# Pair products of layer 0 for three tiles at once, spread over four steps; norms of layers 1 and 2 two steps later

## What is computed

```python
z = jnp.einsum('bmd,bhd->bdmh', x, prev).reshape(b, D, m * h)
t = jnp.einsum('bdc,co->bdo', z, ws[k]) + bs[k]
t = jnp.transpose(t, (0, 2, 1))
norm = jnp.sqrt(jnp.sum(t * t, axis=(-2, -1), keepdims=True))
t = t / norm
logit.append(t)
prev = t
```

## Time and profile before

| | us |
|---|---|
| median of 3 runs | 1061.17 (1060.83 to 1064.76) |
| the profiled execution: its own time | 1062.48 |
| the profiled execution: span | 1060.8 |
| PE busy / PEld busy | 1028.2 / 782.4 |
| DVE busy | 983.6 |
| POOL busy | 865.9 |
| ACT busy | 791.3 |

### The profile page before, as it was taken

How to read it: one execution, slowest core, us unless ns; L and a number is a source line. 1 busy time by engine, 2 the same in 40 slices (tenths; PEclk the granted TensorE clock), 3 DMA queues, 4 the chain that set the end, 5 groups by cost and what they waited for, 6 DMA issues and landing times.

```text
span 1060.8 us, 17970 instructions
## 1 busy us (share of the span) xinstructions
PE 1028.2 (97%) x4320; PEld 782.4 (74%) x4320; DVE 983.6 (93%) x3344; ACT 791.3 (75%) x2655; POOL 865.9 (82%) x729
## 2 busy tenths in 40 slices
PE   2999999999999999999999999999999999999998
PEld 0477777878777787877778787777878777788884
DVE  2589999999999999999999999999999999999993
ACT  3476877868788786868778687777868778788872
POOL 6777988889898888988888898888889888577770
PEclk9999999999999999999999999999999999999999
DMA  5650030302303030120303012030301203000000
GB/s 188 129 143 12 3 88 3 89 2 52 96 4 88 3 87 4 21 71 2 89 3 87 5 28 64 3 89 2 85 7 17 74 3 89 1 1 1 2 1 1
DMA packets 75892, 46.10 MB, mean 43 GB/s; under 512 B 55689, under 2 KB 58633, under 8 KB 75658
## 3 DMA queue, kind: packets, MB, share of 16 engines
q1 hardware_dynamic: 68487, 38.59, 15.2%
q10 hardware_dynamic: 2179, 5.07, 1.4%
q0 software_dynamic: 5120, 1.29, 1.4%
HBM read 42.99 MB, written 1.94 MB: 42 GB/s over the span
## 4 chain that ended last, share of the span: by engine, by line
PE 48%; POOL 19%; DVE 18%; issue 9%; ACT 5%; DMA 1%; POOLq 0%; DVEq 0%; SPq 0%; ACTq 0%
POOL sums L432 14%; DVE sums L946 12%; PE acc L778 8%; PE bank_d L722 7%; PE bank_d L723 6%; PE bank_d L724 6%; PE bank_a L724 6%; PE bank_a L722 6%; PE bank_a L723 6%; POOL gathered L415 5%; ACT scaled L560 4%; DVE bank_d L946 2%; DVE sums L965 1%; ACT sums L560 1%; PE turned L799 1%
## 5 line engine op out<-in xcount | busy, mean ns | idle before, releaser
L432 POOL TENSOR_TENSOR sums<-sums,scaled 128x512 f32<-128x512 f32 (+1 forms) x512 | 645.1, 1262 | 133.4 <-ACT scaled L560 97.4
L946 DVE SCALAR_TENSOR_TENSOR sums<-bank_d,x_col,sums 128x128 f32<-128x128 f32 x2304 | 654.2, 339 | 29.3 <-PE bank_d L724 20.2
L560 ACT ACTIVATE scaled<-bank_a,x_col 128x128 f32<-128x128 f32 x1920 | 551.5, 385 | 139.8 <-PE bank_a L724 132.7
L722 PE MATMUL bank_d<-w_hi,prev_lo 128*128 128x512 f32 x640 | 288.0, 450 | 6.2 <-DVE sums L965 4.7
L722 PE MATMUL bank_a<-w_hi,prev_lo 128*128 128x512 f32 (+1 forms) x640 | 263.9, 412 | 2.6 <-issue 1.3
L724 PE MATMUL bank_d<-w_hi,prev_hi 128*128 128x512 f32 x640 | 252.5, 394 | 0.0
L723 PE MATMUL bank_d<-w_lo,prev_hi 128*128 128x512 f32 x640 | 252.1, 394 | 0.0
L724 PE MATMUL bank_a<-w_hi,prev_hi 128*128 128x512 f32 (+1 forms) x640 | 245.3, 383 | 0.0
L723 PE MATMUL bank_a<-w_lo,prev_hi 128*128 128x512 f32 (+1 forms) x640 | 245.1, 383 | 0.0
L560 ACT ACTIVATE sums<-bank_a,x_col 128x128 f32<-128x128 f32 x512 | 146.1, 369 | 76.8 <-PE bank_a L724 75.9
L415 POOL DMA_INDIRECT gathered<-in_table,idx x160 | 177.2, 1108 | 28.5 <-issue 18.3
(11 more groups left out here) (84 smaller groups left out, 528.2 us busy)
## 6 DMA issues: line engine op xcount, KB each, us to landing
x_pairs<-x_scratch SPq DMA_DIRECT2D x135, 156.0 KB
x_pairs<-x_scratch SPq DMA_DIRECT2D x96, 78.0 KB
gathered<-in_table,idx POOLq DMA_INDIRECT x160
x_sq<-x_scratch SPq DMA_DIRECT2D x32, 64.0 KB
x_pairs<-x_scratch SPq DMA_DIRECT2D x92, 22.0 KB
x_scratch<-gathered SPq DMA_DIRECT2D x16, 72.0 KB
w_raw<-in_w ACTq DMA_DIRECT2D x1, 1024.0 KB, 5.1
w_raw<-in_w ACTq DMA_DIRECT2D x1, 896.0 KB
```

What stands on the lines that cost most here:

```text
L432: nc.gpsimd.tensor_tensor(out=sums[:, n % SUMS, 0:w, :], in0=sums[:, n % SUMS, 0:w, :], in1=scaled[:, a - 1, 0:w, :], op=ALU.add).then_inc ...
L560: op = nc.scalar.activation(to[:, i, :], bank_a[at % A_RING][:, i * UNITS:(i + 1) * UNITS], ACT.Copy, scale=x_of(c, q, a * PER_BANK + i))
L722: nc.tensor.matmul(to, lo, w_h, start=True, stop=False)
L946: nc.vector.scalar_tensor_tensor(out=taken(n, u) if u in LEFT else total, in0=taken(n, u), scalar=x_of(c, q, A_FIELDS + u), in1=total, op0 ...
```

## The change

Layer 0's products are made in two groups of three tiles instead of three groups of two. The first extra row set is loaded a third time to fill the last rows of the third tile, so that each DVE instruction takes all 128 rows. The PE tiles move to other places, the norm of layers 1 and 2 moves from s5/s6 to s7/s0 of the next iteration, and with it `high` and `low` of layer 2's input to (s1, 0); `turn_x` moves to (s2, 9), the reductions of layer 2 on DVE to (s1, 12) and (s1, 15). In chunk 0 all products are made tile by tile, and PE waits for each.

```diff
-EXTRA_PAIRS = [(0, 0, 1, FIELDS - 1), (2, 2 * EXTRA, 2 * EXTRA + 1, 2 * EXTRA - 1)]
+EXTRA_PAIRS = [(0, 0, 1, FIELDS - 1), (3, 2 * EXTRA, 2 * EXTRA + 1, 2 * EXTRA - 1)]
-PAIR_GROUPS = [[0, 1], [2, 3], [4, 5], [6]]
+PAIR_GROUPS = [[0, 1, 2], [3, 4, 5], [6]]
...
-        FINISHES.append((2, _it - 2, (step_at(_it, _q), 3), (step_at(_it, _q + 1), 3)))
+        FINISHES.append((2, _it - 2, (step_at(_it, _q), 3), (step_at(_it, _q + 1), 12 if _it < CHUNKS - 1 else 3)))
...
+    elif _it < CHUNKS:
+
+        NORMS.append((_items, (step_at(_it, 7), 7), (step_at(_it, 7), 3), (step_at(_it + 1, 0), 2)))
     else:
         NORMS.append((_items, (step_at(_it, 5), 7), (step_at(_it, 5), 3), (step_at(_it, 6), 2)))
...
-                    (step_at(_c, 7), 0) if _c < CHUNKS - 1 else (step_at(_c, 5), 3)
+                    (step_at(_c + 1, 1), 0) if _c < CHUNKS - 1 else (step_at(_c, 5), 3)
...
-        _first = (step_at(_it, 0), 2) if _it == 1 else (step_at(_it - 1, 7), 12)
-        _made = [_first, (step_at(_it, 0), 12), (step_at(_it, 1), 12 if _it > 1 else 17), (step_at(_it, 2), 5)]
-        _summed = {(step_at(_it, 0), 5): [0], (step_at(_it, 0), 8): [1], (step_at(_it, 1), 1): [2],
-                   (step_at(_it, 1), 4): [3], (step_at(_it, 2), 1): [4], (step_at(_it, 2), 4): [5],
-                   (step_at(_it, 2), 8): [6]}
+        _i = [step_at(_it, q) for q in range(3)]
+        if _it == 1:
+            _made = [(_i[0], 2), (_i[1], 4), (_i[2], 2)]
+            _summed = {(_i[0], 5): [0], (_i[0], 7): [1], (_i[0], 9): [2]}
+        else:
+            _last = step_at(_it - 1, 7)
+            _made = [(_last, 4), (_i[1], 4), (_i[2], 2)]
+            _summed = {(_last, 7): [0], (_last, 9): [1], (_i[0], 1): [2]}
+        _summed.update({(_i[1], 7): [3], (_i[1], 9): [4], (_i[2], 1): [5], (_i[2], 8): [6]})
...
-TURNS_AT = {((0, 12) if _c == 1 else (step_at(_c - 1, 1), 8)): _c for _c in range(1, CHUNKS)}
+TURNS_AT = {((0, 12) if _c == 1 else (step_at(_c - 1, 2), 9)): _c for _c in range(1, CHUNKS)}
...
-        PAIR_LOADS = [2 * PER_TILE + 3, 2 * PER_TILE + 3, PER_TILE, 0]
+        PAIR_LOADS = [2 * PER_TILE + 4, 2 * PER_TILE + 4, 0]
...
-            if p < 2:
-                tile, _, *partners = EXTRA_PAIRS[p]
-                for i, partner in enumerate(partners):
-                    if tile + i in tiles:
-                        load_rows(queue, c, p, x_rot[PAIR_ROWS:128, tile + i, :], partner, [[2 * ROWS, EXTRA]])
+            tile, _, *partners = EXTRA_PAIRS[p]
+
+            for i, partner in enumerate(partners + partners[:1]):
+                if tile + i in tiles:
+                    load_rows(queue, c, p, x_rot[PAIR_ROWS:128, tile + i, :], partner, [[2 * ROWS, EXTRA]])
...
-                if tile == PAIR_GROUPS[group][0]:
+                if c == 0 and tile in FIRST_SINGLY:
+                    pe.wait_ge(first_pairs_made, FIRST_SINGLY.index(tile) + 1)
+                elif c == 0 or tile == PAIR_GROUPS[group][0]:
                     pe.wait_ge(pairs_made, c * NP + group + 1)
...
-                if c == 0 and p < 2:
+                if c == 0:
+
                     for i in tiles:
                         if i < PICKED:
                             dve.wait_ge(picked, i + 1)
-                        mult = nc.vector.tensor_tensor(out=z0[:, i, :], in0=bank_d[i][:, :] if i < PICKED else x_rot[:, i, :],
-                                                       in1=x_reps[p][:, :], op=ALU.mult)
-                    mult.then_inc(pairs_made, 1)
+                        rows = 128 if i in WITH_EXTRA else PAIR_ROWS
+                        mult = nc.vector.tensor_tensor(out=z0[0:rows, i, :],
+                                                       in0=bank_d[i][0:rows, :] if i < PICKED else x_rot[0:rows, i, :],
+                                                       in1=x_reps[p][0:rows, :], op=ALU.mult)
+                        mult.then_inc(first_pairs_made if i in FIRST_SINGLY else pairs_made, 1)
                     return
-                nc.vector.tensor_tensor(out=z0[0:rows, tiles[0]:tiles[0] + count, :],
-                                        in0=x_reps[min(p, 1)][0:rows, :].unsqueeze(1).to_broadcast([rows, count, ROWS]),
-                                        in1=x_rot[0:rows, tiles[0]:tiles[0] + count, :],
+                nc.vector.tensor_tensor(out=z0[:, tiles[0]:tiles[0] + count, :],
+                                        in0=x_reps[p].unsqueeze(1).to_broadcast([128, count, ROWS]),
+                                        in1=x_rot[:, tiles[0]:tiles[0] + count, :],
                                         op=ALU.mult).then_inc(pairs_made, 1)
```

More of the change, by code:

```diff
@@ L29 @@
 EXTRA = 128 - PAIR_ROWS
-EXTRA_PAIRS = [(0, 0, 1, FIELDS - 1), (2, 2 * EXTRA, 2 * EXTRA + 1, 2 * EXTRA - 1)]
+EXTRA_PAIRS = [(0, 0, 1, FIELDS - 1), (3, 2 * EXTRA, 2 * EXTRA + 1, 2 * EXTRA - 1)]
 SQUARES = PAIR_TILES
-PAIR_GROUPS = [[0, 1], [2, 3], [4, 5], [6]]
+PAIR_GROUPS = [[0, 1, 2], [3, 4, 5], [6]]
 NP = len(PAIR_GROUPS)
+WITH_EXTRA = [first + n for first, _, *partners in EXTRA_PAIRS for n in range(len(partners))]
 PICKED = 3
@@ L279, in cin_kernel @@
         pairs_made = sem("pairs_made")
+        first_pairs_made = sem("first_pairs_made")
         pairs_summed = sem("pairs_summed")
@@ L317, in cin_kernel @@
         y_stored = sem("y_stored")
-        PAIR_LOADS = [2 * PER_TILE + 3, 2 * PER_TILE + 3, PER_TILE, 0]
-        NOT_LOADED = [PER_TILE + 2, 1, 0, 0]
+        PAIR_LOADS = [2 * PER_TILE + 4, 2 * PER_TILE + 4, 0]
+        NOT_LOADED = [PER_TILE + 3, 0, 0]
+        FIRST_SINGLY = [i for tiles in PAIR_GROUPS for i in tiles[:-1]]
         R_STEPS = 4
@@ L506, in _ @@
                 for p in range(NP - 1):
-                    if p < 2:
-                        load_reps(sp, c, p)
+                    load_reps(sp, c, p)
                     if c:
@@ L771, in pair_matmul @@
                     pe.wait_ge(biased, FINISH_NO[0, c - 1] + 1)
-                if tile == PAIR_GROUPS[group][0]:
+                if c == 0 and tile in FIRST_SINGLY:
+                    pe.wait_ge(first_pairs_made, FIRST_SINGLY.index(tile) + 1)
+                elif c == 0 or tile == PAIR_GROUPS[group][0]:
                     pe.wait_ge(pairs_made, c * NP + group + 1)
-                rows = 128 if tile <= EXTRA_PAIRS[-1][0] + 1 else PAIR_ROWS
+                rows = 128 if tile in WITH_EXTRA else PAIR_ROWS
                 if tile == SQUARES:
@@ L791, in pick @@
             def pick(tile):
-                nc.tensor.matmul(bank_d[tile][:, :], turns[:, tile, :], x_rep[0:FIELDS, :],
+                rows = 128 if tile in WITH_EXTRA else PAIR_ROWS
+                nc.tensor.matmul(bank_d[tile][0:rows, :], turns[:, tile, 0:rows], x_rep[0:FIELDS, :],
                                  start=True, stop=True).then_inc(picked, 1)
@@ L807, in _ @@
             keep_busy(4)
-            pe.wait_ge(turns_made, 2 * PICKED)
+            pe.wait_ge(turns_made, PICKED + sum(i in WITH_EXTRA for i in range(PICKED)))
             pe.wait_ge(pairs_loaded[0], pairs_landed(0, 0))
@@ L904, in make_pairs @@
                     dve.wait_ge(pairs_summed, c)
-                rows = 128 if p < 2 else PAIR_ROWS
-                if c == 0 and p < 2:
+                if c == 0:
                     for i in tiles:
```

## The result

| | before | after |
|---|---|---|
| median us (4 executions each) | 1062.62 | 1073.62 (1071.68 to 1075.62) |
| the profiled execution: time / span | 1062.48 / 1060.8 | 1071.68 / 1069.9 |
| DVE busy / POOL busy | 983.6 / 865.9 | 966.6 / 870.5 |

The ratio on record is 1.0113, 95% interval 1.0094 to 1.0132 (the two medians alone give 1.010). That is past the upper end of my range (1061) and on the other side of the sign that I forecast.

What follows compares the result with a forecast made beforehand. PE was taken to bound the kernel, stalling about 1.1 us an iteration. The terms -11.2 - 1.9 - 0.6 + 1.3 gave -12.4 us, so 1050.1 profiled and a median of 1049, range 1046 to 1061.

Steps and rivals of the forecast that it cites:

- Where PE stalled, and why the stall would go: PE loses about 1.1 us an iteration, mostly from s7 to s0, because DVE's slow pair instruction delays its merge.
- Both stalls: PE's stalls from s7 to s0 (0.86) and s1 to s2 (0.15) go: 11.2 and 1.9 us.
- The races: Whether DVE's pair instructions in s7 and s1 get in before POOL's next add; if not, PE waits 0.4 to 0.5.
- A: Both DVE pair instructions get in ahead of POOL's add: 1046 to 1052, the forecast case, chance 0.48.
- B: One pair instruction loses to POOL's add; 0.45 to 0.5 an iteration returns at tile 0 or 3: 1055, chance 0.25.
- C: Both pair instructions lose to POOL's add; 12.4 us come back: 1061, no change, chance 0.10.
- POOL: `low` moves from s7 to s1 and PE time goes to s7: costs 0.1 an iteration, -1.3 us, bounds 0 and 0.8.
- Rival D: The 1.7 us lock and `low` in s1 make POOL late through s2 to s6; s6 wait over 0.8: 1060, chance 0.10.
- Loads: Group 0 grows to 1024 KB, landing 1.9 us before DVE asks in s7; cost nothing.
- rival E: Group 0's loads come late, DVE's queue behind them, in every iteration: 10 us slower, 1071, chance 0.07.
- Start-up: Chunk 0's pair matmuls gain 0 to 0.8, chunk 1 may lose some; together 0, bounds -0.8 and +1.2.
- The floor: PE's work in an iteration without stalls: 61.1 of 62.2 us.

Runs made afterwards that it cites:

- run 3: The kernel before with only the norms of layers 1 and 2 moved as in the change, high and low at (s1, 0): 1060.19 us.
- run 2: The changed kernel with the norms of layers 1 and 2 back at s5/s6 and high and low at (s7, 0): 1073.82 us.
- run 9: The changed kernel with PE's tiles 0 to 2 back in s0 and s1, and keep_busy(8): 1062.94 us.
- run 10: The changed kernel with gathers two in s7, then 2, 1, 2, 2, 1 in s0 to s4, squares at (s2, 5), keep_busy(8): 1053.43 us, ratio 0.9929.
- run 1: The changed kernel with high and low moved from (s1, 0) back to (s0, 3): 1080.93 us.
- run 6: The changed kernel with the squares' instruction at (s2, 5) and ACT's chunk 0 partner loads held until group 0's loads land: 1074.89 us.
- run 5: The changed kernel with gathers 4, 2, 2, 2, 0 in s0 to s4 and six more keep_busy matmuls: 1077.2 us, ratio 1.0146.

## Why the prediction was wrong

*Where PE stalled, and why the stall would go: right in place, incomplete in cause.* Both stalls went, in every iteration but the two with late loads. But I gave the 0.86 to the product instruction of s7; run 3 removes it by moving the norms alone. DVE's lag at s7 came from the norm work of s6, on which the slow instruction stood. The 0.86 an iteration was real and belonged to the smaller part of the change.

*The races (A against B and C): right.* The instruction of s7 took 1.76, that of s1 2.28, no PE wait for products in a steady iteration.

*POOL: the step that failed.* It stood as -1.3 us (0.1 an iteration, bounds 0 and 0.8). It measured 1.3 an iteration, 13 times the value and above the upper bound. I wrote that 1.7 us of PE's time go to s7 "against about 3 us that it idled there; it has nothing left", and then priced what that means at 0.1. POOL's work between s0 and s6 grew by the 1.3 of `low`, and the 1.7 us of PE's time were taken out of the same stretch and given to one in which POOL waits for ACT. Run 2 takes the first half back, run 9 the second, and each has 23 waits for POOL where the change has 45. Rival D had the place (waits of DVE for POOL through s2 to s6), the sign and nearly the size (0.85 an iteration against 1.3), and 0.10 of the chance. Its own sign would have missed it: the wait at s6 is 0.47, not over 0.8, because the lateness shows at four steps. What I had against it, that three locks become two, was beside the point: runs 9 and 10 keep the long locks and have few of the waits. The Trainium skill (SBUF — State Buffer, "SBUF: two separate sides") has an instruction of VectorE with two SBUF inputs and one of GpSimd that reads SBUF block each other for a whole instruction. The rows agree, but DVE's instructions cost POOL 2.2 us in that stretch before and 2.05 after, so the lock is no more than an addition here. Whether a part of the 0.4 that run 9 leaves belongs to it was not run.

*`low` in s1 and the squares:* no item's place within the stretch is the cause. Runs 1, 6 and 5 move one kind each and get 62.65, 62.5 and 62.77. What helped was to take work out of the stretch (run 2, `low` to s7; run 10, two gathers to s7 and one fewer in s1) or to give it PE's time back (run 9).

*Loads: right for 11 of 13 iterations (1.9 us to spare), wrong for two that I did not look at.* At the end of iteration 3 another eight loads stand in the same queue: 4.7 us. The other is 0.46 late. The rival E had the mechanism, but as one of every iteration. A queue has to be read over the whole span, not in a typical stretch.

*Start-up: taken as 0, bounds -0.8 and +1.2; T0 0.55 later, iteration 1 0.65 later*, 1.2 in all, the upper bound, and that in the fastest execution; three others with this start-up had T0 4 to 5 us later still. The gain of 0.8 was never there. I read the 12 pair matmuls at 32.83 as waiting for both products, but PE's own picks ran until 32.81 before, and until 32.64 after, with the matmuls at 32.57 right behind them.

*The sum.* The floor was right: I had 61.1, iterations without lateness take 61.15 to 61.17. Against the forecast of -12.4 the span rose by 9.2. Of the 21.6 between them, the stalls for POOL are 13.7 (about 15 us, 1.3 in each of twelve iterations but for two with less, where the sum had 1.3); iteration 3 is 4.7, the context 1.4, the start-up 1.2, the late load of iteration 7 0.5; the rest is the tail and rounding.

## What to carry to other kernels

When work on the bounding engine is moved to another step, ask of every *following* engine what it did in the stretch that loses the time: PE's extra work is another engine's chance to catch up, and it is worth most where that engine's queue is full. Look for the cheapest part alone first; here the norms took away the large stall and a small shift of two DVE instructions (a pair instruction and `turn_x`) the rest, while the larger product groups, most of the edit, gave nothing. And read the queue of loads in the iterations that differ, since one late load costs as much as many small waits.
